# The last stage of an attention and mixture-of-experts layer: residual rows read earlier, gather indices taken from the slot table

## The reference

```python
x = layernorm(x + attention(x))                 # x: 8 batches x 512 rows x 512
...
router_logits = x @ gate_w.T                    # x now (4096, 512), 8 experts
topk_w, topk_i = jax.lax.top_k(softmax(router_logits), 2)
topk_w = topk_w / jnp.sum(topk_w, axis=-1, keepdims=True)
out = jnp.zeros_like(x)
for e in range(8):
    w_e = jnp.sum(jnp.where(topk_i == e, topk_w, 0.0), axis=-1)
    gated = silu(x @ w_gate[e]) * (x @ w_up[e])  # 512 -> 352
    out = out + w_e[:, None] * (gated @ w_down[e])
return layernorm(x + out)
```

## Time and profile before

| | |
|---|---|
| median of 3 runs | 2114.99 us (2112.66 to 2120.06) |
| profiled execution | 2115.3 us |
| its span, first to last instruction | 2113.5 us |
| busy: TensorE, VectorE, ScalarE, GpSimd | 81%, 65%, 55%, 28% of the span |
| DMA queues of the span: software (GpSimd), SyncE's, ScalarE's | 6.8%, 39.8%, 3.4% of sixteen engines |
| moved | 319.56 MB, mean 151 GB/s |

### The profile page before, as it was taken

One profiled execution on the slowest core, in us unless ns is written; L12 is line 12 of the kernel. 1 busy time (PEld: TensorE's weight loads), 2 busy tenths in 40 slices (PEclk: granted clock), 3 DMA queues, 4 the chain that ended last, 5 costly groups with the idle time before them and its releaser, 6 DMA issues. The chain is left out here.

```text
span 2113.5 us, 37090 instructions
## 1 busy us (share of the span) xinstructions
PE 1703.5 (81%) x9698; PEld 1257.0 (59%) x9699; DVE 1381.8 (65%) x3222; ACT 1168.4 (55%) x3375; POOL 592.8 (28%) x504
## 2 busy tenths in 40 slices
PE   4578899899799899899989889670899999999500
PEld 3456556556566655655655655430799999999500
DVE  2579978978878878888888887713433333333366
ACT  2468877778778777777876876720122222222133
POOL 2232322422332322332232241104533332000265
PEclk7799999999999999999999999875899999999755
DMA  7965464564564564573573573105434243223298
GB/s 259 293 181 162 131 189 128 167 180 128 162 184 142 158 172 141 147 203 113 157 217 118 147 216 81 74 26 188 134 119 120 77 140 94 79 85 98 82 285 269
DMA packets 142981, 319.56 MB, mean 151 GB/s; under 512 B 16720, under 2 KB 19408, under 8 KB 140656
## 3 DMA queue, kind: packets, MB, share of 16 engines
q1 hardware_dynamic: 113424, 241.90, 39.8%
q0 software_dynamic: 14432, 48.64, 6.8%
q10 hardware_dynamic: 14976, 27.27, 3.4%
HBM read 216.03 MB, written 109.05 MB: 154 GB/s over the span
## 5 line engine op out<-in xcount | busy, mean ns | idle before, releaser
L772 ACT ACTIVATE expd<-S,neg_max 128x128 f32<-128x128 f32 (+3 forms) x1024 | 530.7, 537 | 163.8 <-DVE neg_max L923 162.0
L923 DVE TENSOR_REDUCE neg_max<-S 128x2 f32<-128x768 f32 (+3 forms) x384 | 399.3, 1040 | 202.1 <-PE S L625 201.7
L954 DVE SCALAR_TENSOR_TENSOR mixed<-expd,rho 128x384 f32<-128x384 f32 (+3 forms) x512 | 328.8, 662 | 0.1
L621 PE MATMUL S<-kT,qT 128*128 128x256 f32 (+2 forms) x1024 | 283.3, 379 | 36.6 <-DMA qT<-parts_rows 20.5
L636 PE MATMUL PTp<-ident,mixed 128*128 128x128 f32 x1280 | 215.7, 284 | 82.2 <-DVE mixed L954 78.1
L784 ACT ACTIVATE probsT<-PTp 128x512 f32<-128x512 f32 (+2 forms) x384 | 205.3, 535 | 123.3 <-PE PTp L636 121.8
L672 PE MATMUL tail<-wo,ctxT 128*128 128x512 f32 x512 | 248.8, 614 | 23.4 <-ACT ctxT L820 13.4
L621 PEld LDWEIGHTS S<-kT,qT 128*128 128x128 f32 x1024 | 164.5, 196 | 137.2 <-issue 95.9
L1357 ACT ACTIVATE xT_hi<-xTp 128x512 fp32r<-128x512 f32 x72 | 43.1, 598 | 365.1 <-DVE yo L1533 349.2
L513 POOL TENSOR_TENSOR swapped<-swapped,rope_t 128x512 f32<-128x512 f32 x80 | 103.2, 1290 | 489.0 <-DVE swapped L916 489.0
L772 ACT ACTIVATION_READ_ACCUMULATOR expd<-S,neg_max 128x1 f32 x1024 | 218.9, 214 | 0.0
(11 more groups left out here) (209 smaller groups left out, 3627.9 us busy)
## 6 DMA issues: line engine op xcount, KB each, us to landing
qT<-parts_rows SPq DMA_DIRECT2D x256, 256.0 KB, 4.5
parts_rows<-parts SPq DMA_DIRECT2D x160, 256.0 KB, 2.0
wqk<-wqk_split SPq DMA_DIRECT2D x75, 512.0 KB, 5.8
xin<-expert_in_rows SPq DMA_DIRECT2D x72, 256.0 KB, 3.0
expert_out_rows<-yo ACTq DMA_DIRECT2D x72, 256.0 KB, 3.2
kT<-parts_rows SPq DMA_DIRECT2D x64, 256.0 KB, 4.2
x<-in_x SPq DMA_DIRECT2D x8, 1024.0 KB, 7.1
x_rows<-x SPq DMA_DIRECT2D x8, 1024.0 KB, 7.0
```

What stands on the lines that cost most here:

```text
L621: nc.tensor.matmul(S[s % 2][:, k * slot:k * slot + w], qT[kv % 2][:, 2 * h + c, i * P:(i + 1) * P], kT[kv][:, c, 0:w], start=(k % per_bank ...
L772: ex = nc.scalar.activation(expd[s % 3][:, k * slot:k * slot + w], S[s % 2][:, k * slot:k * slot + w], ACT.Exp, bias=neg_max[s % 3][:, k:k ...
L923: nc.vector.tensor_reduce(neg_max[s % 3][:, 0:k], v, AX, ALU.max, negate=True).then_inc(max_ready, 1)
L954: ins = nc.vector.scalar_tensor_tensor(out=mixed[sl % 3][:, a * 256:a * 256 + w], in0=e2, scalar=rr[:, i, h:h + 1], in1=e1, op0=ALU.mult, ...
```

## The change

What it does:

- EARLY grows from 8 to 16. SyncE's reads of `x_early` now stand beside the last 16 pairs of tiles, and cover the first 16 tiles of the combine stage. ROUND = 8 is the new name of the ring's size.
- The raw weight buffers `w_raw` are allocated for the rest of the program. When GpSimd has split expert 6 and issued expert 7's weights, it issues eight reads of residual rows into the buffer of expert 6, and eight more into that of expert 7 once that is split: tiles 16 to 31 (`x_raw`).
- In the combine stage SyncE has nothing to do. VectorE waits once for all `x_raw`, at tile 16.
- The gathers take their index from a column of `out_slots`; `cidx`, its copies and `idx_ready` go.
- GpSimd's and VectorE's programs of the stage are written out for all 32 tiles. ScalarE's keeps its loop.

```diff
--- before.py
+++ after.py
@@ -43,7 +43,8 @@
 MT += MT % 2
 IC = [(o, min(P, I - o)) for o in range(0, I, P)]
 GE = 32
-EARLY = 8
+EARLY = 16
+ROUND = 8
 SLOTS = 3
 WCOLS = DC * 2 * I + len(IC) * D
 WFULL = DC * 2 * I + 2 * D
@@ -129,12 +130,14 @@
                         ident, ones, slots, wts, msum)
         x_early = sbk("x_early", [P, EARLY, D])
+        w_raw = [sbk(f"w_raw{r}", [P, WCOLS]) for r in range(2)]
+        x_raw = [w[:, 0:ROUND * D].rearrange("p (t d) -> p t d", t=ROUND) for w in w_raw]
+        x_raw_in = keep.enter_context(nc.semaphore("x_raw_in"))
         x_early_in = keep.enter_context(nc.semaphore("x_early_in"))
         with ExitStack() as weights:
             w_hi = weights.enter_context(nc.sbuf_tensor("w_hi", [P, SLOTS * WCOLS], F32R))
             w_lo = weights.enter_context(nc.sbuf_tensor("w_lo", [P, SLOTS * WCOLS], F32R))
-            w_raw = [weights.enter_context(nc.sbuf_tensor(f"w_raw{r}", [P, WCOLS], F32)) for r in range(2)]
             ew_in = [weights.enter_context(nc.semaphore(f"expert_w_in{e}")) for e in range(E)]
             def load_weights(queue, e):
@@ -147,9 +150,9 @@
             plan_block(nc, plan_d, load_weights, xs_dram, ones, msum, slots, out_slots,
                        exp_tab, row_tab, slot_tab, past_tab)
-            expert_block(nc, w_hi, w_lo, w_raw, ew_in, load_weights, xs_dram, ys_dram, x1_dram, x_early, x_early_in, ident,
+            expert_block(nc, w_hi, w_lo, w_raw, ew_in, load_weights, xs_dram, ys_dram, x1_dram, x_early, x_early_in, x_raw, x_raw_in, ident,
                          exp_tab, row_tab, slot_tab, past_tab)
-        combine_block(nc, x1_dram, ys_dram, out_slots, wts, x_early, x_early_in, out)
+        combine_block(nc, ys_dram, out_slots, wts, x_early, x_early_in, x_raw, x_raw_in, out)
 def attention_block(nc, x, xT_d, wT_d, wv_d, wo_d, lam_d, gnw_d, gnb_d, gate_d, rope_d,
@@ -1271,7 +1274,7 @@
             link(nc.vector.tensor_copy(slot_tab[:], ek[:]))
-def expert_block(nc, w_hi, w_lo, w_raw, ew_in, load_weights, xs_dram, ys_dram, x1_dram, x_early, x_early_in, ident,
+def expert_block(nc, w_hi, w_lo, w_raw, ew_in, load_weights, xs_dram, ys_dram, x1_dram, x_early, x_early_in, x_raw, x_raw_in, ident,
                  exp_tab, row_tab, slot_tab, past_tab):
     with ExitStack() as ctx:
         def sb(name, shape, dt=F32):
@@ -1421,6 +1424,11 @@
                 pool.sem_inc(w_ready, 1)
                 if e + 1 < E:
                     load_weights(nc.gpsimd, e + 1)
+                if e >= E - 2:
+
+                    t0 = EARLY + ROUND * (e % 2)
+                    for t in range(ROUND):
+                        pool.dma_start(x_raw[e % 2][:, t, :], x1_dram[(t0 + t) * P:(t0 + t + 1) * P, :]).then_inc(x_raw_in, 16)
         @block.tensor
         def _(pe):
@@ -1559,7 +1567,7 @@
             take_y(MT - 1, 1)
-def combine_block(nc, x1_dram, ys_dram, slots, wts, x_early, x_early_in, out):
+def combine_block(nc, ys_dram, slots, wts, x_early, x_early_in, x_raw, x_raw_in, out):
     NTT = N // P
     with ExitStack() as ctx:
@@ -1569,11 +1577,9 @@
         def sem(name):
             return ctx.enter_context(nc.semaphore(name))
-        G = EARLY
+        G = ROUND
         ya = [sb(f"ya{r}", [P, TOPK, D]) for r in range(G)]
-        x_late = sb("x_late", [P, NTT - G, D])
         res = [sb(f"res{r}", [P, D]) for r in range(G)]
-        idx = [sb(f"cidx{r}", [P, TOPK], U32) for r in range(G)]
         bs = [sb(f"bs{r}", [P, 6]) for r in range(G)]
         mv = [sb(f"cmv{r}", [P, 2]) for r in range(G)]
         sd = [sb(f"sd{r}", [P, 1]) for r in range(G)]
@@ -1581,8 +1587,6 @@
         nb = [sb(f"nb{r}", [P, 1]) for r in range(G)]
         eps_t = sb("ceps", [P, 1])
         gathered = [sem(f"gathered{r}") for r in range(G)]
-        x_in = [sem(f"cx_in{r}") for r in range(G)]
-        idx_ready = sem("cidx_ready")
         first_added = sem("first_added")
         summed = sem("summed")
         bn_done = sem("bn_done")
@@ -1603,35 +1607,17 @@
         rounds = NTT // G
         out_f = out.rearrange("b t d -> (b t) d")
-        @block.sync
-        def _(sp):
-            with nc.sync.Fori(1, rounds) as m:
-                for r in range(G):
-                    t = m * G + r
-                    sp.wait_ge(idx_ready, t + 1)
-                    sp.dma_start(x_late[:, bass.ds(t - G, 1), :].rearrange("p a d -> p (a d)"),
-                                 x1_dram[bass.ds(t * P, P), :]).then_inc(x_in[r], 16)
-
         @block.gpsimd
         def _(pool):
-            def gather(t, r, wait):
-                if wait:
+            for t in range(NTT):
+                r = t % G
+                if t >= G:
                     pool.wait_ge(summed, t - G + 1)
                     apart(pool)
-                nc.gpsimd.tensor_copy(idx[r][:], slots[:, bass.ds(t, 1), :].rearrange("p a k -> p (a k)")) \
-                  .then_inc(idx_ready, 1)
-                pool.wait_ge(idx_ready, t + 1)
-                apart(pool)
                 for k in range(TOPK):
                     nc.gpsimd.indirect_dma_start(ya[r][:, k, :], None, ys_dram,
-                                                 bass.IndirectOffsetOnAxis(ap=idx[r][:, k:k + 1], axis=0)) \
+                                                 bass.IndirectOffsetOnAxis(ap=slots[:, t, k:k + 1], axis=0)) \
                       .then_inc(gathered[r], 16)
-
-            for r in range(G):
-                gather(r, r, False)
-            with nc.gpsimd.Fori(1, rounds) as m:
-                for r in range(G):
-                    gather(m * G + r, r, True)
         @block.scalar
         def _(act):
@@ -1665,18 +1651,17 @@
             nc.vector.memset(eps_t[:], EPS).then_inc(eps_set, 1)
             def weights(t):
-                return wts[:, bass.ds(t, 1), :].rearrange("p a k -> p (a k)")
+                return wts[:, t, :]
             def add_first(m, r):
                 t = m * G + r
                 dve.wait_ge(gathered[r], 32 * (m + 1))
-                if isinstance(m, int):
-                    xr = x_early[:, r, :]
-                else:
-                    xr = x_late[:, bass.ds(t - G, 1), :].rearrange("p a d -> p (a d)")
-                    dve.wait_ge(x_in[r], 16 * m)
+                if m > 0:
                     dve.wait_ge(stored[r], 16 * m)
+                if t == EARLY:
+                    dve.wait_ge(x_raw_in, 16 * 2 * G)
+                xr = x_early[:, t, :] if t < EARLY else x_raw[(t - EARLY) // G][:, r, :]
                 nc.vector.scalar_tensor_tensor(out=res[r][:], in0=ya[r][:, 0, :], scalar=weights(t)[:, 0:1], in1=xr,
                                                op0=ALU.mult, op1=ALU.add).then_inc(first_added, 1)
@@ -1703,26 +1688,17 @@
                 nc.vector.scalar_tensor_tensor(out=nb[r][:], in0=mv[r][:, 0:1], scalar=-1.0, in1=rs[r][:],
                                                op0=ALU.mult, op1=ALU.mult).then_inc(nb_ready, 1)
-            def step(m, r):
-
-                t = m * G + r
-                one, two = not isinstance(m, int) or r >= 1, not isinstance(m, int) or r >= 2
-                add_first(m, r)
-                if one:
-                    moments(t - 1, (r - 1) % G)
-                add_second(t, r)
-                if two:
-                    inverse(t - 2, (r - 2) % G)
-                stats(t, r)
-                if two:
-                    offset(t - 2, (r - 2) % G)
-
             dve.wait_ge(x_early_in, 16 * EARLY)
-            for r in range(G):
-                step(0, r)
-            with nc.vector.Fori(1, rounds) as m:
-                for r in range(G):
-                    step(m, r)
+            for t in range(NTT):
+                add_first(t // G, t % G)
+                if t >= 1:
+                    moments(t - 1, (t - 1) % G)
+                add_second(t, t % G)
+                if t >= 2:
+                    inverse(t - 2, (t - 2) % G)
+                stats(t, t % G)
+                if t >= 2:
+                    offset(t - 2, (t - 2) % G)
             moments(NTT - 1, G - 1)
             for t in (NTT - 2, NTT - 1):
                 inverse(t, t % G)
```

## The result

The changed kernel takes 2103.81 us (median of 7 runs, 2088.99 to 2106.91) against 2115.51 for the kernel before beside it (7 runs, 2111.88 to 2120.06). The ratio is 0.9926, with an interval of 0.9899 to 0.9954: 10 to 21 us are gained, where the forecast said 22.8. The direction is right. As to size the answer is divided. By the ratio the gain is 15.7 us, two thirds of the forecast's, and taken off the 2115.3 from which I predicted it gives 2099.6, inside the range of 2086 to 2101.5. The profiled execution, 2088.99 us against a span of 2087.1, is the fastest of the seven and lies inside it too; the plain median, 2103.81, lies 2.3 us above its upper end. So two questions are left: which part of the change gives the gain, and what puts five of the other six executions 10 to 18 us above the profiled one.

The account below looks back on a forecast made before the run. GpSimd's issue and the DMA engines were taken as equal floors of the combine stage. 32 tiles at 2.70 us save 21.8 us, the earlier start 1.0: 2115.3 - 22.8 = 2092.5 us, range 2086 to 2101.5.

Parts of the forecast that it names:

- second floor of the same height: Combine stage: DMA engines need 3.23 us a tile at full engines, 3.43 at 0.94 busy, level with GpSimd's issue.
- Part 1: GpSimd in the combine stage: dropping 32 index copies saves 0.7 us a tile; first gather starts 1.0 us earlier.
- Part 2: Combine stage: 24 residual reads go, leaving a DMA floor of 2.53 to 2.90 us a tile, middle 2.71.
- The stretch of the gathers: Combine stage: gathers lengthened by full DMA engines, 0.075 us each, kept as 2 x 0.075 a tile.
- Rival A: Combine stage: emptier DMA engines end the gathers' lengthening; pace 2.54 to 2.60, 2087.4 to 2089 us; chance 20%.
- Part 3: VectorE in the combine stage: 2.32 us a tile, within 0.2 us of GpSimd but not the bound.
- Parts 4 to 6: Residual reads beside the experts, and rows held in raw weight buffers: priced at nothing; bursts at most 4 us.
- Rivals B to E: DMA alone binds (26%); bursts cost up to 4 us (4%); table stride slows gathers (3%); code fetches (3%).
- E: Combine stage: fetching written-out code stops VectorE and GpSimd, slower than before, 2123 to 2132 us; chance 3%.

## Why the prediction was right or wrong

**What bounds: half right.** GpSimd's issue was the bound, as its idle times showed. That the DMA engines were a second floor of the same height is false. With the reads gone and the copies kept the ratio is 1.0008; with the reads kept and the copies gone it is 0.9944 and they carry 345 GB/s. What failed is the step from the earlier trace rows: I added packet times of crowded and less crowded stretches as if they were fixed costs, and took 0.94 busy for a ceiling. They were 0.94 busy because nobody asked for more. I wrote that 0.95 was as far as the engines got, but the trace of before has ten microseconds that say otherwise:

```profile
2050.00:2060.00 10.00, 0.00 (x0) 0.00 (x0) 7.20 (x18) 3.32 (x6) 6.64 (x10) 0.50 0.99 332
```

The 358 GB/s at which, by the Trainium skill (DMA: Bandwidth & Descriptors, "Where 436 GB/s comes from"), the HBM side binds, left out of the sum, come nearer to what the experiment reached, but the trace does not show them as a limit either: it has 345 over 31 us and 398 over 13. What I had worked out from that figure, that the DMA engines would be no limit after the change, came true all the same.

**Part 1, the copies: right.** 0.7 us a tile was promised and 0.62 measured (3.40 to 2.78), with a bare pace of 2.52 where no gather is held, for 2.54 foretold. Of the 1.0 us at the start 0.4 came: the stage's first instruction of GpSimd now comes 0.7 us later behind the last `yo`.

**Part 2, the reads: the conclusion wrong, the number right by chance.** The middle of 2.71 was made of a DMA floor that no experiment finds. The forecast's 2.70 stood because part 1 and the stretch made 2.69 by themselves.

**The stretch of the gathers: right in size, wrong in cause.** I kept the 0.15 us a tile of before; it became 0.26, since VectorE now adds during a larger share of the time. Rival A promised that the stretch would go with the crowding. It grew as the crowding fell. Rival A's pace, 2.54 to 2.60, needs an operand in PSUM: then it is 2.52.

**Part 3, VectorE: right.** It takes 2.24 us a tile where its input is there (2069.17 less 2066.91 is 2.26), for 2.32 foretold, and isn't the bound. **Parts 4 to 6: right**: the bursts take GpSimd 4.27 and 4.25 us to issue; for the rest, TensorE's 10.00 of 10 us beside both bursts, the split of expert 7 with 40.28 us of idle time before it, and this one wait of TensorE from 1730 on, as in the earlier trace rows:

```profile
PE Y L1483 <- DVE hT_lo L1533: 2.4, 1, 2.4
```

The slowest `xin` now lands in 8.1 us, and nobody waits for it. **Rivals B to E did not come**: no gather waited for `summed` for long (1.8 us in all; 5.8 to 6.2 with the slow stretch), and the slow stretch, which looks most like E, begins at tile 14 (counted from 0) in two profiles and at 18 in the third, so that it hangs on no place in the code.

**The sum.** First gather to the end of the last: 88.7 us against 86.4. Two terms were absent. One is the race at the experts' start, 8 us by chance in both kernels, which my profile of before had lost. I took the profiled 2115.3 as the typical time because it lay at the median, and didn't ask whether an execution could come out otherwise. The other is the slow stretch, 7 to 10 us. Together they are large enough for executions 10 to 18 us above the profiled one, but which of the two sat in which unprofiled execution is argued, not shown. There is a third source of scatter that has nothing to do with the change: up to the last padding write all fourteen profiles run the same code, and it takes 1459.8 to 1472.0 us, on the third chip alone 1459.8 to 1467.0. So a difference of a few microseconds between two kernels is safer read in the stage than in the whole time. On the fourth chip the ratio of 0.9906 holds the forecast's 0.9892 in its interval; in the first comparison it lies just outside.

**What stays open.** The slow stretch was in all three fast-paced profiles on the first chip, in none of eight on the others, and neither in the kernel before nor in the one with copies. What holds VectorE's own signals there I can't say. The counts don't exclude that it is the chip, or the hour.

## What to carry to other kernels

Where two resources seem to be floors of the same height, undo the change by halves: one pair of runs said that all the gain came from 32 small copies on the issuing engine, and that 6 MB of traffic moved out of the stage gave none that could be measured. The busy share of DMA engines says that they have work, not that they can't take more. When an instruction is sometimes longer, look at what the other engine was doing in the moment when it began, before blaming a resource that is full on average. And send a control with every comparison.

## What the runs showed that I had not expected

- Whether a gather of 0.95 us takes up to 1.48 is decided by a tenth of a microsecond of alignment with VectorE's adds. All of it together was 4.9 us in the kernel before and 8.4 in the one after; 32 tiles multiplied by the identity on an idle TensorE (36 instructions, 32.9 us busy, in 2010 to 2060) take it away and bring 5 to 9 us.
- The same subtraction on VectorE, 128x3840 with two inputs in SBUF, took 13.2 us or 5.2, and 4.76 with GpSimd kept off; GpSimd's cast beside it 3.94 or 7.91. A kernel can have a scatter of 8 us from one such race.
- The DMA engines moved 345 GB/s over 31 us at 0.99 busy, of these 13 us at 398, and 331 beside TensorE at full work.
